# The first two heads of a latent-attention block: gate transposes, gather products and key transposes in another order

## The reference

```python
qc = layernorm(x @ W_cq, q_norm_w, q_norm_b)              # 192 wide
q_nope, q_pe = split(qc @ W_q)                            # per head 128 + 64
k_pe, kv_nope = split(x @ W_ckv)                          # per head 64 + 128
kvp = layernorm(kv_nope, ...) @ W_kv                      # k_nope, v
scores = q @ k.T / sqrt(192), causal; probs = softmax(scores); attn = probs @ v
gate = (x @ W_ig).T                                       # 8 rows of 1024 tokens
_, top_idx = top_k(gate, 8)                               # 8 tokens for each of 8 index heads
sel = take(x @ W_ip, top_idx)                             # 64 gathered rows
io = mean(softmax(sel@W_sq @ (sel@W_sk).T / sqrt(128)) @ (sel@W_sv) @ W_io)
attn = attn + repeat(io);  out = attn @ W_o
```

## Time and profile before

| | |
|---|---|
| runs | 671.64 us median (671.07 to 673.1) |
| profiled execution | 671.92 us, of which the span from first to last instruction 670.0 us |
| mean granted TensorE clock | 0.987 of full |
| PE busy | 637.3 us (95%) |
| PE weight loads busy | 568.4 us (85%) |
| DVE busy | 447.7 us (67%) |
| ACT busy | 398.8 us (60%) |
| POOL busy | 374.5 us (56%) |
| chain that ended last | PE 71%, ACT 13%, DVE 10%, issue 6% |

### The profile page before, as it was taken

One profiled execution on the slowest core, in us unless ns is written; L12 is line 12 of the kernel. 1 busy time (PEld: TensorE's weight loads), 2 busy tenths in 40 slices (PEclk: granted clock), 3 DMA queues, 4 the chain that ended last, 5 costly groups with the idle time before them and its releaser, 6 DMA issues.

```text
span 670.0 us, 13275 instructions
## 1 busy us (share of the span) xinstructions
PE 637.3 (95%) x4096; PEld 568.4 (85%) x4096; DVE 447.7 (67%) x1228; ACT 398.8 (60%) x904; POOL 374.5 (56%) x332
## 2 busy tenths in 40 slices
PE   8788999999999999999999999999999999789996
PEld 6678888898889888888889888988898888689895
DVE  5967467665766666675756675657665758797664
ACT  5875347754774575656664666466754777436552
POOL 5964278454654565466728473738454735371664
PEclk9988999999999999999999999999999999889998
DMA  8306232510371037103600352114410482000001
GB/s 236 120 2 151 70 78 60 124 57 1 96 164 55 0 94 164 55 0 94 160 36 23 86 119 53 55 47 114 97 55 0 116 245 70 10 1 1 1 18 48
DMA packets 23550, 49.84 MB, mean 74 GB/s; under 512 B 3168, under 2 KB 16352, under 8 KB 21600
## 3 DMA queue, kind: packets, MB, share of 16 engines
q1 hardware_dynamic: 22144, 47.82, 27.9%
q10 hardware_dynamic: 1376, 1.64, 0.7%
HBM read 16.94 MB, written 1.05 MB: 27 GB/s over the span
## 4 chain that ended last, share of the span: by engine, by line
PE 71%; ACT 13%; DVE 10%; issue 6%; POOL 1%; ACTq 0%; POOLq 0%; DVEq 0%
PE J L892 6%; PE J L858 6%; PE J L860 5%; PE J L859 5%; PE J L915 5%; ACT kvraw L1306 5%; PE SC L882 4%; PE SC L879 4%; PE SC L880 4%; PE SC L883 4%; PE SC L881 4%; ACT Pb L1208 3%; PE J L912 3%; PE J L911 2%; PE J L907 2%
## 5 line engine op out<-in xcount | busy, mean ns | idle before, releaser
L1208 ACT ACTIVATE Pb<-SC,nm 128x128 f32<-128x128 f32 (+7 forms) x128 | 94.8, 741 | 58.0 <-DVE nm L1427 57.1
L1358 DVE TENSOR_TENSOR PTl<-J,PTh 128x512 fp32r<-128x512 f32 (+1 forms) x192 | 101.0, 550 | 30.8 <-ACT PTh L1191 30.6
L1427 DVE CUSTOM_DVE_ANT_0 SC<-SC,mask 128x128 f32<-128x128 f32 (+7 forms) x128 | 97.1, 759 | 22.3 <-PE SC L883 21.3
L1191 ACT ACTIVATE PTh<-J 128x512 fp32r<-128x512 f32 (+1 forms) x192 | 87.6, 491 | 19.6 <-PE J L892 19.4
L892 PE MATMUL J<-ident,Pb 128*128 128x128 f32 x576 | 87.6, 278 | 9.5 <-DVE qcs L1358 3.1
L892 PEld LDWEIGHTS J<-ident,Pb 128*128 128x128 f32 x576 | 66.0, 141 | 17.1 <-DVE qcs L1358 3.3
L1358 DVE TENSOR_TENSOR ATl<-J,ATh 128x512 fp32r<-128x512 f32 (+1 forms) x34 | 22.4, 659 | 75.8 <-ACT ATh L1191 75.8
L879 PE MATMUL SC<-KNh,QNh 128*128 128x128 f32 (+2 forms) x192 | 70.3, 366 | 1.6 <-DVE KNl L1358 1.6
L882 PE MATMUL SC<-KK,QS 128*128 128x128 f32 (+2 forms) x192 | 66.3, 345 | 0.0
L881 PE MATMUL SC<-KNh,QNl 128*128 128x128 f32 (+2 forms) x192 | 66.0, 344 | 0.0
L880 PE MATMUL SC<-KNl,QNh 128*128 128x128 f32 (+2 forms) x192 | 66.0, 344 | 0.0
(11 more groups left out here) (316 smaller groups left out, 1993.2 us busy)
## 6 DMA issues: line engine op xcount, KB each, us to landing
KK<-RK SPq DMA_DIRECT2D x30, 512.0 KB, 6.3
QS<-RQh SPq DMA_DIRECT2D x15, 256.0 KB, 7.8
QS<-RQl SPq DMA_DIRECT2D x15, 256.0 KB, 6.7
KX<-KX SPq DMA_DIRECT2D x14, 256.0 KB, 2.4
QX<-QX SPq DMA_DIRECT2D x14, 256.0 KB, 2.4
r_kv<-in_W_ckv SPq DMA_DIRECT2D x7, 384.0 KB, 4.3
r_o<-in_W_o SPq DMA_DIRECT2D x18, 128.0 KB, 3.1
r_qn<-in_W_qT SPq DMA_DIRECT2D x16, 128.0 KB, 3.1
```

The lines of the kernel that those rows point to most:

```text
L1191: return act.activation(o, i, ACT.Copy)
L1208: act.activation(Pb[i % 2][:, w], SC[i % 2][:, s], ACT.Exp, bias=nm[:, i % 2:i % 2 + 1], scale=-1.0, accum_out=sm[:, b, i:i + 1]).then_inc ...
L1358: dve.tensor_tensor(o, i, h.bitcast(F32), ALU.subtract).then_inc(done[kind], 1)
L1427: dve.tensor_tensor_reduce(out=SC[i % 2][:, s], in0=SC[i % 2][:, s], in1=mask[:, 128 * (7 - i):S], scale=-SCALE, scalar=HIGH, op0=ALU.add, ...
```

## The change

The lists are reordered in three regions, two copies change engine, and the banks fall differently:

1. Prologue and first query tiles. `wb` goes ahead of `qm` 2, 3 on PE and ahead of the statistics on DVE; the last statistics step (`kvs` 3) leaves the prologue and stands behind the second row maximum. The gate transposes (`side` 0, 1) go from behind `qk` 2 to behind `qk` 0. Their copies to `gT` become a step of their own, `gcopy`, that DVE does behind `qk` 2. The first probability transposes stand ahead of `exp` 1.
2. Head 0, query tiles 6 and 7. `side` 2 goes from ahead of `t(0, 5)` to behind the key transposes `kt` 1; `side` 3, 4 go behind `wo` 0, 1. The two `skip`s go from the front of the list to its end.
3. Head 1. The key transposes `kt` 1 of the next head go from behind `pv` and `t(h, 4)` to ahead of them.

```diff
         FIRST_HEAD = [
-            ("qk", 0, 0), ("exp", 0, 0), ("qmb", 0, 2), ("kvag", 0, 1),
-            ("qk", 0, 1), ("qmb", 0, 3), ("exp", 0, 1), *t(0, 0),
+            ("qk", 0, 0), ("side", 0, 0), ("side", 0, 1), ("exp", 0, 0), ("qmb", 0, 2),
+            ("qk", 0, 1), ("kvs", 0, 3), ("kvag", 0, 1), ("qmb", 0, 3), *t(0, 0), ("exp", 0, 1),
             ("rk", 0, 1),
-            ("qk", 0, 2), ("side", 0, 0), ("side", 0, 1), ("rkl", 0, 1), ("exp", 0, 2), ...
+            ("qk", 0, 2), ("gcopy", 0, 0), ("gcopy", 0, 1), ("rkl", 0, 1), ("exp", 0, 2), ...
...
-            ("qk", 0, 6), ("side", 0, 2), ("exp", 0, 6), *t(0, 5), ("kt", 1, 1), ("wosp", 2, 0), ("wqn", 2, 0), ("wqp", 1, 0), ("kv", 1, 0),
-            ("side", 0, 3), ("side", 0, 4), ("wo", 0, 0), ("wo", 0, 1),
+            ("qk", 0, 6), ("exp", 0, 6), *t(0, 5), ("kt", 1, 1), ("side", 0, 2), ("wosp", 2, 0), ("wqn", 2, 0), ("wqp", 1, 0), ("kv", 1, 0),
+            ("wo", 0, 0), ("wo", 0, 1), ("side", 0, 3), ("side", 0, 4),
...
         def head_steps(b, first, last):
...
+                add(5, first, ("kt", n, 1))
                 add(5, True, ("pv", h, int(last)), *t(h, 4))
-                add(5, first, ("kt", n, 1))
...
-                  each("kt", 0) + each("kv", 3) + each("qm", 2, 3) + each("wb", 0))
+                  each("kt", 0) + each("kv", 3) + each("wb", 0) + each("qm", 2, 3))
...
-                   each("kvs", 2) + each("qms", 3) + each("kvs", 3) + each("wb", 0))
+                   each("wb", 0) + each("kvs", 2) + each("qms", 3))
...
-        FIRST[0:0] = [("skip", 0, 0)] * (-len(banked(FIRST)) % NB)
+        assert len(banked(FIRST)) % NB == 0, len(banked(FIRST))
...
-                    if kind == "side" and c in (0, 1):
-                        act.wait_ge(ready["side"], c + 1)
-                        act.wait_ge(head1_lo, 1)
-                        act.wait_ge(rq0_ready, 1)
-                        copy(gT[:, half(c)], o[0:8, :]).then_inc(done["side"], 1)
...
+                    if kind == "gcopy":
+                        dve.wait_ge(ready["side"], c + 1)
+                        dve.wait_ge(head1_lo, 1)
+                        dve.wait_ge(rq0_ready, 1)
+                        dve.tensor_copy(gT[:, half(c)], o_of("side", c)[0:8, :]).then_inc(done["side"], 1)
```

More of the change, by code:

```diff
@@ L317, in attention_and_mlp @@
         FIRST_HEAD = [
-            ("qk", 0, 0), ("exp", 0, 0), ("qmb", 0, 2), ("kvag", 0, 1),
-            ("qk", 0, 1), ("qmb", 0, 3), ("exp", 0, 1), *t(0, 0),
+            ("qk", 0, 0), ("side", 0, 0), ("side", 0, 1), ("exp", 0, 0), ("qmb", 0, 2),
+            ("qk", 0, 1), ("kvs", 0, 3), ("kvag", 0, 1), ("qmb", 0, 3), *t(0, 0), ("exp", 0, 1),
             ("rk", 0, 1),
-            ("qk", 0, 2), ("side", 0, 0), ("side", 0, 1), ("rkl", 0, 1), ("exp", 0, 2), ("qn", 0, 1), ("qp", 0, 1), ("qps", 0, 1),
+            ("qk", 0, 2), ("gcopy", 0, 0), ("gcopy", 0, 1), ("rkl", 0, 1), ("exp", 0, 2), ("qn", 0, 1), ("qp", 0, 1), ("qps", 0, 1),
             ("ropeq", 0, 1), ("kvn2", 0, 1), *t(0, 1),
@@ L327, in attention_and_mlp @@
             ("qk", 0, 5), ("pv", 0, 0), ("exp", 0, 5), ("top8", 0, 3), *t(0, 4),
-            ("qk", 0, 6), ("side", 0, 2), ("exp", 0, 6), *t(0, 5), ("kt", 1, 1), ("wosp", 2, 0), ("wqn", 2, 0), ("wqp", 1, 0), ("kv", 1, 0),
-            ("side", 0, 3), ("side", 0, 4), ("wo", 0, 0), ("wo", 0, 1),
+            ("qk", 0, 6), ("exp", 0, 6), *t(0, 5), ("kt", 1, 1), ("side", 0, 2), ("wosp", 2, 0), ("wqn", 2, 0), ("wqp", 1, 0), ("kv", 1, 0),
+            ("wo", 0, 0), ("wo", 0, 1), ("side", 0, 3), ("side", 0, 4),
             ("qk", 0, 7), ("side", 0, 5), ("exp", 0, 7), ("kv", 1, 1), ("side", 0, 6), ("qn", 1, 1), ("kpe", 1, 0), ("kpe", 1, 1),
-            ("ropek", 1, 0), *t(0, 6), ("side", 0, 7), ("kv", 1, 2), ("side", 0, 8), ("kv", 1, 3), ("side", 0, 9)]
+            ("ropek", 1, 0), *t(0, 6), ("side", 0, 7), ("kv", 1, 2), ("side", 0, 8), ("kv", 1, 3), ("side", 0, 9), ("skip", 0, 0), ("skip", 0, 0)]
         def head_steps(b, first, last):
@@ L521, in attention_and_mlp @@
         bank_of = {s[0:3]: s[3] for s in numbered(PRO_PE)}
-        bank_of.update({s[0:3]: s[3] for s in numbered(FIRST) if s[0] in ("qp", "qps") and s[1] == 0})
+        bank_of.update({s[0:3]: s[3] for s in numbered(FIRST) if s[0] in ("qp", "qps", "side") and s[1] == 0})
         def placed(steps):
```

## The result

The kernel after takes 679.16 us (median of four runs, 679.02 to 680.41) against 671.59 for the kernel before in the same session: 1.011 times as long, with a 95% interval of 1.0095 to 1.0125. Forecast were 674.6 and a range up to 676.4: the sign was right, the size was not, and the time lies outside the range. The profiled execution took 679.22 us with a span of 677.4, against 670.0 before.

What follows compares the result with a forecast made beforehand. PE (TensorE), busy 95% of the span, was taken as the bound, so only its idle times and clock count. Terms -2.4 + 2.9 + 0.8 + 1.7 = +3.0 us on the profiled 671.92 gave 674.9, forecast 674.6 as median; range 669.5 to 676.4.

Steps and rivals of the forecast that it cites:

- first tiles: First query tiles of head 0: `tc` starts earlier, `qn` waits for `qcs`, `qp` for the gate copy; 2.4 us gained.
- tile 6: Head 0, query tile 6: `kv` waits for `PTl` of `t(0, 5)` and the clock falls (1.7); 2.9 us lost, clock share 0.85 to 2.55.
- key transposes, head 1: Head 1: `qn` of head 2 waits for `KNl` instead of `ATl`; 0.8 us lost.
- their clock: Head 1: the clock falls behind the 2.3 us idle time ahead of `qn` of head 2; 1.7 us lost, bounds 0 and 1.7.
- Rival D: Tile 6: `t(0, 5)` evicted early, `kv` doesn't wait, clock stays up; 667.6, or 669.3 with head 1's drop; chance 0.20.
- rival C: First tiles: idle times of 1.5 and 0.7 us count together, the clock falls, some 1.3 us lost; 675.9; chance 0.12.
- rival B: Head 1: the clock holds because work in line cuts the 2.3 us idle time; 672.9, no change; chance 0.22.

Runs made afterwards that it cites:

- e3: Kernel after with the key transposes of head 1 again behind `pv` and `t(h, 4)`: 676.07 us, 1.007 of the kernel before.
- e4: Kernel after with tile 6, head 1 and the two skips' place ahead of `side` 9 restored, leaving only the first region of the change: 670.59 us, 0.9978.
- e7: e4 with `side` 3, 4 behind `wo` as in after, and `side` 2 behind the first `kv` of the next pair: 675.9 us, 1.0052.
- e13: The kernel after measured once more, no edit, beside e10 to e12: 677.87 us, 1.0101 of the kernel before.
- e10: e4 with only the two skips put back behind `side` 9, at the end of the list as in after: 674.37 us, 1.0039.
- e1: Kernel after with the two skips ahead of `side` 9 instead of behind it: 675.13 us, 1.0045 of the kernel before.
- e12: Kernel before with only the key transposes of head 1 moved ahead of `pv` and `t(h, 4)`: 673.2 us, 1.0024.
- e2: Kernel after with `side` 2 ahead of `t(0, 5)` and `side` 3, 4 ahead of `wo` again: 673.91 us, 1.0035 of the kernel before.
- e6: e4 with `side` 3, 4 behind `wo` 0, 1 as in after, `side` 2 staying ahead of `t(0, 5)`: 671.01 us, 0.9989.
- e9: e4 with the two gate copies done by ACT instead of DVE, at the same place of the list: 668.46 us, 0.9955.
- e11: e9 with `qcs` ahead of the aggregate on DVE and, on ACT, `QNh` ahead of `exp` 2 and `rkl`: 668.76 us, 0.9958.

## Why the prediction was wrong

| step | forecast | measured in after | clean size |
|---|---|---|---|
| first tiles | -2.4 | -0.8 | -1.9 (e3, e4, e7) |
| tile 6 | +2.9 | +3.7 | +3.7 (after, e3, e13) |
| skips at the end | none | +3.5 | 3.44 (e10), 3.48 (e1) |
| key transposes, head 1 | +0.8 | +0.8 | 0.78 (e1, e12), 0.76 (e3) |
| their clock | +1.7 | 0 | 0 in four profiles, a drop in e12 |
| start, last pair | 0 | -0.5, +0.7 | spread |

**The step that failed is a term that the sum does not have.** The prediction followed the banks that "are dealt anew" only at tile 6 and at `qn` of head 2. It left out the third place, behind the two `skip`s, and said of the whole of head 1 before `qn` that "PE's work before that is the same". The matmuls are the same, but one of them now waits: PE idles 2.43 us for `side` 9, and the clock falls behind it. This one term, put at nothing, is 3.5 us; e1 takes it away and e10 puts it back, each alone. Added to the forecast it gives 674.6 + 3.5 = 678.1, between the two medians of after (677.87 and 679.16). That it fits so well is partly chance, as the other errors nearly cancel: 1.7 of clock in head 1 did not come, while the first tiles gained 1.6 less than forecast (0.5 of the gain itself, 1.2 of clock, 18.79 less 17.62) and tile 6 cost 0.8 more.

**Tile 6** came as described: `kv` waits 2.59 for `PTl`, and L943 no longer waits for `i8d`. `kv` starts at 60.87, which is 62.15 when the fifth scores are laid over those of before, exactly as forecast. Too small was the clock's share. It was priced at one drop of 1.7, but the clock was still low in the second stretch (63:67 at 0.62), so the work behind `kv` lost 0.5 x 2.1 up to 63 and 0.38 x 4 behind it, 2.6 us in all. That lies at the upper bound that was given (2.55). A drop is not worth 1.7 everywhere either: behind the wait for `i8d` it fell in before, e4 and e12 (rest of head 0: 37.78, 38.12, 37.76) and held in e2, e6, e9 and e10 (37.51, 37.85, 37.57, 37.59), a difference of 0.6 at most. Where it held, PE waited 0.58 to 0.63 more for `PTl` behind `kv`, as the L948 row of e2 shows, so part of what the clock gave was lost again. Rival D did not occur: `PTl` came no sooner.

**First tiles.** The route was right (`tc` early, `qn` waiting for `qcs`, `qp` for the copy), and so in the main was the copy's price: each takes 0.67, and the second starts 0.60 behind the first, against the 0.6 that was taken and the estimate of 0.53. The clean gain is 1.9 instead of 2.4. Most of the missing 0.5 is there at `qn` already: it starts at 34.26 on a start that is 0.5 earlier, 34.78 on before's scale, where the forecast has 34.4, because the row maximum, the statistics and the aggregate ahead of `qcs` are together some tenths later. `qp` then starts at 36.68 on that scale, forecast 36.25.

In after itself the clock fell as well, as rival C has it: from `qp` to the end of `qps` PE took 39.76 - 36.16 = 3.60 us, in e3 39.06 - 36.62 = 2.44. But C's reason, two idle times that count together, is not what is seen. The last matmul of `qn` (L1051 at 35.27) already takes 0.56 where it takes 0.40 in e3, so the clock was down before the second idle time began; e6, e10 and e13 are alike, and only in e1 and e2 (35:36 at 0.95 and 0.91) did it fall within the second. It fell in 6 of the 10 profiles with the wait of 1.8 ahead of `qn` (after, e1, e2, e6, e10, e13) and held in e3, e4, e7 and e9. C had a chance of 0.12.

**Head 1.** The 0.8 of waiting is exact. The drop behind it did not come in after (115:119 at 1.00), nor in e1, e2 and e13: rival B's condition, though no work cut the idle time. It came in e12 behind 2.27. The rule I read from before's rows, a drop behind each idle time of 1.86 us or more, doesn't hold. TensorE: Matmul & The Clock Gate of the Trainium skill, section "What you observe", has the point at which the clock comes up, early in steady matmul work, move by 0.5 us either way between runs. That is about the rise; no run here measures it. Of the fall the runs show that it is not settled by the length of the wait: 2.25 us held and 2.27 lost.

What stays open: why one execution keeps its clock and the next loses it, and why half clock lasted so long in e7. The cost of the clock in a given place can be read only after the fact.

## What to carry to other kernels

Where buffers are dealt in turn, list for every product who held its buffer before, with the count and not only the semaphore, and compare the two lists from the first moved step to the end: two fillers that compute nothing, moved past a single step, cost 3.5 us, nearly as much as the costliest move of steps with work (3.7). When a copy changes engine, ask which engine stands in the chain to the next wait; here the new order of the first tiles was worth 2.6 us with the copies left on ACT (16.93 in e9 against 19.55) and 1.9 with them on DVE (17.62 in e4). Price a wait of around 2 us on PE as itself plus a clock drop that may or may not come, and give the range both.

## What was not expected of the hardware

- The same wait goes both ways. Behind the wait for `i8d` of 2.02 to 2.05 us the clock fell in before, e4 and e12 and held in e2, e6, e9 and e10, and it held behind 2.74 in e11. In the first tiles it fell in after behind 1.78 and held in e3 behind 1.79. Behind the 1.86 of the last pair it fell in before and after and held in e13.
- The time of one kernel therefore spreads with its clock: e4's twelve executions run from 668.47 us (mean granted clock 0.993) to 674.35 (0.984).
- Half clock can last through continuous work: in e7 PE was busy 11.75 of the 12 us from 61 to 73 and had 0.57, 0.50 and 0.50, for the most part in matmuls of 64 columns. Whether their size is the reason wasn't tried.
